# Layer 2's routing stage: the up product of batch 1 cut into eight pieces between the routings, and the counting product set inside its down product

## What is computed

```python
# feed-forward (x1 = x + attention)
h = _layernorm(x1, ln2_g, ln2_b)
x1 = x1 + jax.nn.gelu(h @ W_ff1, approximate=False) @ W_ff2     # 256 -> 1024 -> 256
# experts
logits = jnp.einsum('nh,eh->ne', xt, router_w)                  # 4096 tokens, 8 experts
probs = jax.nn.softmax(logits, axis=-1)
scores, expert_idx = jax.lax.top_k(probs, TOP_K)                # TOP_K = 2
scores = scores / jnp.sum(scores, axis=-1, keepdims=True)
h = jnp.einsum('nh,ehd->end', xt, up_proj)
hidden = jax.nn.silu(h[..., :D]) * h[..., D:]
out_e = jnp.einsum('end,edh->enh', hidden, down_proj)
out = jnp.einsum('ne,enh->nh', gate, out_e)
```

## Time and profile before

| what | value |
|---|---|
| median of 3 runs | 3460.21 us (3457.18 to 3463.37) |
| the profiled execution | 3464.72 us, of which the span is 3463.0 us |
| TensorE busy | 3044.8 us, 88% of the span |
| VectorE, ScalarE, GpSimd busy | 2107.1, 1393.6, 1390.0 us |
| mean granted TensorE clock | 0.927 of full speed |
| layer 2's second half | about 2191 to 2719 us of the span |

### The profile page before, as it was taken

How to read it: one execution, slowest core, us unless ns; L and a number is a source line. 1 busy time by engine, 2 the same in 40 slices (tenths; PEclk the granted TensorE clock), 3 DMA queues, 4 the chain that set the end, 5 groups by cost and what they waited for, 6 DMA issues and landing times. The chain is left out here.

```text
span 3463.0 us, 46451 instructions
## 1 busy us (share of the span) xinstructions
PE 3044.8 (88%) x14629; PEld 1851.4 (53%) x14629; DVE 2107.1 (61%) x6568; ACT 1393.6 (40%) x3126; POOL 1390.0 (40%) x981
## 2 busy tenths in 40 slices
PE   7849995999699997999999998699999668898888
PEld 4427773666355554444444544565666445555554
DVE  4569998995544424466666654522222468888777
ACT  4425664453366652344343433122332323333331
POOL 1426100655244440122122212133005598988883
PEclk9879997999899998999999998789999879999999
DMA  5577553332300001000000000312223200000000
GB/s 186 180 253 227 177 153 110 110 110 73 126 1 1 1 1 43 7 19 7 13 19 19 19 13 13 131 57 84 92 84 92 80 0 7 7 7 7 7 7 13
DMA packets 138092, 221.08 MB, mean 64 GB/s; under 512 B 12800, under 2 KB 106240, under 8 KB 137088
## 3 DMA queue, kind: packets, MB, share of 16 engines
q1 hardware_dynamic: 99040, 146.92, 12.8%
q0 software_dynamic: 18432, 50.36, 4.6%
q10 hardware_dynamic: 20384, 20.84, 1.8%
HBM read 107.45 MB, written 110.62 MB: 63 GB/s over the span
## 5 line engine op out<-in xcount | busy, mean ns | idle before, releaser
L2313 DVE CUSTOM_DVE_ANT_0 a_ps_s<-a_ps_s,a_hide_row,a_fmax 128x384 f32<-128x384 f32 (+3 forms) x512 | 249.4, 555 | 170.3 <-PE a_ps_s L2020 170.1
L2225 POOL TENSOR_SCALAR_AFFINE_SELECT a_probs<-a_probs 128x512 f32<-128x512 f32 x128 | 79.7, 635 | 565.4 <-ACT a_probs L2502 565.4
L3594 POOL TENSOR_TENSOR c_prod<-c_att,c_v 128x2048 f32<-128x2048 f32 x64 | 287.3, 4529 | 29.1 <-DVE c_att L3654 29.1
L3594 POOL TENSOR_TENSOR c_prod<-c_q,c_k 128x2048 f32<-128x2048 f32 x64 | 286.5, 4508 | 16.5 <-ACT c_k L4005 13.5
L1521 POOL TENSOR_TENSOR a_probs<-a_probs,a_causal 128x512 f32<-128x512 f32 (+1 forms) x96 | 157.2, 1649 | 216.1 <-ACT a_probs L1750 216.1
L1750 ACT ACTIVATE a_probs<-a_ps_s 128x512 f32<-128x512 f32 (+1 forms) x384 | 170.7, 538 | 120.5 <-PE a_ps_s L1390 120.4
L2502 ACT ACTIVATE a_probs<-a_ps_s 128x512 f32<-128x512 f32 (+1 forms) x384 | 171.9, 538 | 91.1 <-PE a_ps_s L2042 90.5
L3428 PE MATMUL c_side<-c_w_e,c_h2T 128*128 128x512 f32 x448 | 203.4, 609 | 4.1 <-DVEq L3801 4.1
L703 PE MATMUL p_side<-p_w_expert,p_sortedT 128*128 x636 | 171.2, 392 | 0.0
L2881 POOL DMA_INDIRECT b_rows<-y_scratch,b_slot_int x64 | 62.7, 980 | 239.8 <-issue 239.8
L3654 DVE TENSOR_REDUCE c_att<-c_prod 128x128 f32<-128x2048 f32 x64 | 143.3, 2278 | 19.8 <-POOL c_prod L3594 18.0
(11 more groups left out here) (508 smaller groups left out, 7231.2 us busy)
## 6 DMA issues: line engine op xcount, KB each, us to landing
p_sorted_in<-sorted_scratch SPq DMA_DIRECT2D x39, 512.0 KB
y_scratch<-p_y_out SPq DMA_DIRECT2D x39, 512.0 KB
sorted_scratch<-all_zero ACTq DMA_DIRECT2D x1, 12160.0 KB, 57.8
sorted_scratch<-all_zero SPq DMA_DIRECT2D x1, 9088.0 KB, 30.7
b_sorted_in<-sorted_scratch SPq DMA_DIRECT2D x17, 512.0 KB, 4.5
y_scratch<-b_y_out SPq DMA_DIRECT2D x17, 512.0 KB, 3.2
sorted_scratch<-all_zero ACTq DMA_DIRECT2D x1, 8192.0 KB, 31.9
all_x_res<-x SPq DMA_DIRECT2D x8, 512.0 KB, 4.9
```

Of the source, the lines that this page charges most:

```text
L2313: last = nc.vector.tensor_tensor_reduce(out=there, in0=there, in1=hide_row[:, (TT - 1 - t) * P:], scale=HD ** -0.5, scalar=fmax[i % 2][:, ...
L3594: nc.gpsimd.tensor_tensor(out, left[:, heads].broadcast_to([P, HALF, HEADS, HD]), right.broadcast_to([P, HALF, HEADS, HD]), ALU.mult).then ...
```

## The change

Batch 1's up product is cut into eight pieces of two products (one PSUM bank each), and piece b stands behind `route(b - 1)` in the routing loop; ScalarE's gelu of piece b stands behind `row_columns(b)`. `turn_h(2)` moves ahead of the counting product, and the counting product moves from behind `ff_up(1)` to the middle of `ff_down(1)` (after two of its four row tiles). VectorE normalises batch 2 before it picks experts, rather than between the gates and `place`. On ScalarE `h_columns(2)` moves ahead of the gates' exponential. On GpSimd the reciprocal root of batch 3 comes after 16 scatters, not 18.

```diff
-            def ff_up(i):
+            def ff_up(i, first=0, end=NF):
...
-                for k in range(KD):
-                    pe.wait_ge(*side.when_freed("hn", i, k))
-                for n in range(NF):
+                if first == 0:
+                    for k in range(KD):
+                        pe.wait_ge(*side.when_freed("hn", i, k))
+                for n in range(first, end):
...
-            def ff_down(i):
+            def ff_down(i, first=0, end=TT):
...
-                for t in range(TT):
+                for t in range(first, end):
...
-                last.then_inc(ff2_done, 1)
+                if end == TT:
+                    last.then_inc(ff2_done, 1)
...
                 turn_rows(b)
                 if b:
                     route(b - 1)
+                ff_up(1, b, b + 1)
             route(B - 1)
-            ff_up(1)
+            turn_h(2)
+            ff_down(1, 0, 2)
             count()
-            for i in range(1, B):
-                if i > 1:
-                    ff_up(i)
+            ff_down(1, 2, TT)
+            for i in range(2, B):
+                ff_up(i)
...
                 scatter(t)
-                if t == 8:
+                if t == 7:
                     ln.pool_rstd(pool, 3)
...
             h_moments(2)
+            normalise_h(2)
             dve.wait_ge(ones_set, ONE + 1)
             pick_experts()
             gates()
-            normalise_h(2)
             place()
...
             for b in range(B):
                 row_columns(b)
+                gelus(1, b, b + 1)
+            h_columns(2)
             act.wait_ge(route_step, ONE + 13)
```

More of the change, by code:

```diff
@@ L2694, in ff_up @@
                     last.then_inc(side.filled("ff", i, n), 1)
-            def ff_down(i):
+            def ff_down(i, first=0, end=TT):
                 if i == 0:
                     pe.wait_ge(ff2_in, ONE + DMA)
-                pe.wait_ge(ff_added, ONE + i)
-                for n in range(NF):
-                    pe.wait_ge(*side.when_freed("ff", i, n))
-                for t in range(TT):
+                if first == 0:
+                    pe.wait_ge(ff_added, ONE + i)
+                    for n in range(NF):
+                        pe.wait_ge(*side.when_freed("ff", i, n))
+                for t in range(first, end):
                     for n in range(NF):
@@ L3112, in h_columns, with gelus @@
                                          scale=cols[:, k, 0:1]).then_inc(side.freed("hn", i, k), 1)
-            def gelus(i):
-                act.wait_ge(ff2_done, ONE + i)
-                for n in range(NF):
+            def gelus(i, first=0, end=NF):
+                if first == 0:
+                    act.wait_ge(ff2_done, ONE + i)
+                for n in range(first, end):
                     act.wait_ge(*side.when_filled("ff", i, n))
```

## The result

The changed kernel takes 3452.41 us (median of 11 runs, 3446.06 to 3455.59) against 3462.16 us for the kernel before, run beside it (11 runs, 3457.18 to 3466.67). The ratio is 0.9971 with a 95% interval of 0.9962 to 0.9979, that is 10.0 us less by the ratio, between 7.3 and 13.2. The prediction was 8.2 us less, 3452.0.

What follows compares the result with a forecast made beforehand. The prediction took the routing loop to be bound by TensorE's low clock and the stretch behind it by GpSimd's roots behind scatters. 8.9 us gained less 0.7 lost made 8.2 less than 3460.2: 3452.0 us, range 3446 to 3460.

Steps and rivals of the forecast that it cites:

- Step 1: Routing loop: a turn of transposes, router and piece takes 4.5 us, eight turns 36.0 us (35.0 to 37.6).
- Step 2: Routing loop: TensorE's full clock holds with 2.64 us of transposes and router between pieces; if not, a turn costs 8.5 us.
- The first rival: Routing loop: the clock falls now and then, 4.0 us more per low turn; 3456 us, chance 0.09.
- The rule against it: Routing loop: the Trainium skill says transposes do not count as a busy engine for the clock, so it would fall.
- Step 3: Last router to counting product: 7.9 us instead of 15.8, so the counting product comes 8.9 us earlier (7.3 to 10.1).
- T: Time of the counting product's start, on which the stretch to the experts hangs: 2286.00 us before, 2277.1 forecast.
- Step 4: Counting product to experts: GpSimd's pace stays, so TensorE's 0.94 + 7.0 us less work is given back in two waits.
- Step 5: Behind the longer waits before turn_h(3) and turn_h(4): low clock costs 0.7 us, bounds 0 and 1.9.
- Step 6: Sorted tiles and after the experts: edits cost nothing, 17.4 us of cover as before; what follows moves as a whole.
- within 0.2%: Whole kernel: the time differs from the kernel before by no more than 0.2% (6.9 us); chance 0.28.
- the slow case: Routing loop: the clock falls and stays down, 3465 to 3484 us; chance 0.05, with slower given as 0.06.

Runs made afterwards that it cites:

- up_ahead: Changed kernel with batch 1's whole up product and its gelus ahead of the routing loop, not in pieces inside it; ratio 1.0018 to the kernel before.
- by_two: Changed kernel with two pieces of the up product together in every second turn of the routing loop; ratio 0.9998 to the kernel before.
- turn_thrice: Kernel before with each transpose of the routing loop done three times into the same place; ratio 0.9993 to the kernel before.
- count_late: Kernel before with only the counting product moved, behind turn_h(2) and half of ff_down(1); ratio 1.0022 to the kernel before.
- before_roots: Kernel before with the roots of batches 3, 4 and 5 after 10, 32 and 56 scatters, not 18, 42 and 64; ratio 0.9975.
- roots_early: Changed kernel with the roots of batches 3, 4 and 5 after 6, 28 and 50 scatters, not 16, 42 and 64; ratio 0.9927 to the kernel before.
- count_first: Changed kernel with the counting product right behind the last router product, ahead of turn_h(2) and all of ff_down(1); ratio 0.9983 to the kernel before.
- count_first_exp: Changed kernel with the counting product right behind the last router product and, on ScalarE, the gates' exponential ahead of h_columns(2); ratio 0.9970 to the kernel before.

## Why the prediction was right

The change gained 10.0 us by the runs and 10.5 in the stretch, for the 8.2 forecast. That 3452.0 and the measured 3452.41 lie 0.4 us apart is luck: the forecast started from a median of 3460.2 us for the kernel before, which beside the changed kernel took 3462.16, and this hid the 2 us.

- **Step 1, a turn of 4.5 us.** Measured 4.38, the lower bound of the prediction; the two semaphore waits that I had added cost nothing. Over eight turns that is 1.0 us.
- **Step 2, the clock holds.** It did, at 1.00 (first window above), and `up_ahead` shows that this is the gain: without the pieces in between the same work takes 17.6 us more. The argument from layer 3 was right, but I did not see how near an edge lay: I had taken the 7.2 us of the earlier trace rows as a time that the clock stands, and in `by_two`, with 5.75 us of thin work in a row, it falls each round and most of the gain is lost. The first rival (falls now and then) may have been closer than its 0.09 said; in the changed kernel no fall was seen.
- **The rule against it.** It was right to let outweigh it; `turn_thrice` shows the same in a loop of its own.
- **Step 3, T 8.9 us earlier.** From E to the counting product it was 52.6 us and is 42.8: 9.9, inside the bounds. The picking was covered with 2.1 us to spare, where I said 2.5.
- **Step 4, GpSimd keeps its pace.** `turn_h(3)` came at T + 31.6 (said 30.9) and waited 9.97 us (said 9.2); `turn_h(4)` at T + 65.8 (said 66.1). `count_late` and the column S to experts, 101.9 to 104.4 us in the ten profiles with the roots in their old places, in which TensorE has up to 8 us more or less to do behind the counting product, show that the roots behind the scatters set the time; `before_roots` and `roots_early`, which move them, bring it to 93.5 and 92.4. That it is S and not T that counts, `count_first` taught; in the changed kernel they move together (7.77 us). The prediction called these 7.77 us all `place`; 1.07 of them are the counting product, which is why they grew to 8.80 when it ran at the low clock in `count_first_exp`.
- **Step 5, the price of the longer waits.** This term had the wrong sign: I took 0.7 us of loss, and T to the experts was 0.7 us shorter (110.4 for 111.1). The low clock at the first wait lasted much longer than I thought, 13.4 us with the wait, and the down product took 16.02 us. (It costs a little more than I had reckoned, too: two batches at the full clock with no wait are 28.6 us apart in `before_roots`, not 28.9.) But it ran in the slack before `turn_h(4)`, so that the wait there was 2.65 us and not the predicted 5.2. Behind `turn_h(4)` the clock then did not fall, and batch 5 came so early that it too waited for its root (1.24 us).
- **Step 6.** The stretch is 10.5 us shorter and the runs 10.0 (7.3 to 13.2), so nothing was seen to be lost behind the experts.

In the stretch the sum was off by 2.3 us: 1.0 in step 1 and 1.4 in step 5, less rounding. The 8.2 us of the forecast lie within the interval of the measurement too. In the chances, the parts listed for "within 0.2%" add up to 0.29 and the slow case to 0.05, where the text has 0.28 and 0.06.

## What to carry to other kernels

When TensorE runs a chain of small operations at the low clock, more dense work between them can make the chain itself faster; spread it evenly, since the same work in lumps lost most of the gain here. Before counting saved work as a gain, look for the queue that paces the stretch: here 8 us of TensorE's work taken out behind the counting product were worth nothing, as it waited for tiny operations behind long scatters. Moving three of these was worth 9 us in the kernel before and, by the profile, 14 in the changed one, whose own gain was 10. And an engine's list in order can tie a step to one that it has no need of (the exponential behind `h_columns(2)`), which costs nothing until the order elsewhere changes.

## What the runs showed that I had not expected

- With 16 transposes more in it, a turn of the routing loop took 4.36 us for 5.01.
- A wait of 5.69 us before the counting product doubled the product's own time (1.19 us for 0.59; 2.1 us from its start to VectorE's first copy, for 1.1).
- The changed kernel, profiled twice, took 1064.3 and 1060.9 us from its first expert tile to the end of the span, with the same instructions. The expert stage is alike in both (221.2 and 221.0 us), so the 3 us lie behind it, in the rest of layer 2 and in layers 3 and 4; their cause is open. It is why changes of 1 us are read from the stretch here and not from the time.
